# Where the node sums are zeroed, and a memset behind every second edge gather: a graph and expert kernel on one core

## The reference, cut to what matters

```
x = x + gnn(layernorm(x), z, src, dst, sh, ele)
    h   = linear(x_n) * z ;  s = linear_skip(x_n) * z
    w   = silu(ele @ fc_w0) @ fc_w1                # 50000 x 256, one row per edge
    mid = products of w, h[src] and sh             # 50000 x 512
    y   = segment_sum(mid, dst)                    # 3125 x 512
    out = c_s * s + c_x * linear2(y) * z
x = x + ffn(layernorm(x))
    shared expert (gelu) on all nodes + the two best of 8 experts, weighted
```

## Time and profile before

| | us |
|---|---|
| median of three runs | 1373.57 (1373.14 to 1381.37) |
| the profiled execution | 1377.12 |
| its span, first to last instruction | 1375.2 |
| first gather to last gather | 65.19 to 799.03 |
| mean granted TensorE clock | 0.895 of full |

### The profile page before, as it was taken

One profiled execution on the slowest core, in us unless ns is written; L12 is line 12 of the kernel. 1 busy time (PEld: TensorE's weight loads), 2 busy tenths in 40 slices (PEclk: granted clock), 3 DMA queues, 4 the chain that ended last, 5 costly groups with the idle time before them and its releaser, 6 DMA issues. The chain is left out here.

```text
span 1375.2 us, 31654 instructions
## 1 busy us (share of the span) xinstructions
PE 1175.3 (85%) x8904; PEld 1008.7 (73%) x8904; DVE 769.0 (56%) x1951; ACT 726.8 (53%) x2357; POOL 634.2 (46%) x695
## 2 busy tenths in 40 slices
PE   5667888788888888878878887999799999999993
PEld 4445666667766666656756677999799999999993
DVE  5634555555555545545555567644357666676652
ACT  4535766566756656655746666445344444444431
POOL 4565555545545545445444510355224444455443
PEclk9869888878979888878888898999899999999997
DMA  8652323323323333323333336223324344443222
GB/s 292 191 163 82 103 72 114 115 82 105 99 92 105 95 99 111 105 86 110 97 92 93 98 109 216 89 77 112 102 59 101 54 97 105 108 105 73 43 40 31
DMA packets 86943, 141.64 MB, mean 103 GB/s; under 512 B 14926, under 2 KB 65422, under 8 KB 86480
## 3 DMA queue, kind: packets, MB, share of 16 engines
q0 software_dynamic: 31840, 67.39, 20.1%
q1 hardware_dynamic: 51104, 69.90, 15.2%
q10 hardware_dynamic: 3920, 3.41, 0.8%
HBM read 99.48 MB, written 30.95 MB: 95 GB/s over the span
## 5 line engine op out<-in xcount | busy, mean ns | idle before, releaser
L748 POOL DMA_INDIRECT x_wlo<-h_tab,src_sb x392 | 376.5, 960 | 365.0 <-DVE hot L897 155.3
L779 ACT ACTIVATE hots<-hot,sh_all 128x64 f32<-128x64 f32 x1568 | 383.9, 336 | 0.0
L1103 PE MATMUL psY<-prod,hots 128*64 128x128 f32 x2352 | 345.9, 311 | 13.1 <-issue 12.4
L1103 PEld LDWEIGHTS psY<-prod,hots 128*64 128x64 f32 x2352 | 312.9, 160 | 28.0 <-issue 28.0
L1099 PE MATMUL psY<-prod,hots 128*64 128x256 f32 x784 | 273.4, 472 | 10.4 <-issue 10.1
L925 DVE SCALAR_TENSOR_TENSOR y_sb<-psY,mask,y_sb 128x256 f32 x196 | 85.7, 478 | 264.9 <-remote 235.0
L1864 ACT ACTIVATE q_hf<-q_psA,x_b 128x256 f32<-128x256 f32 x232 | 110.2, 475 | 186.7 <-PE q_psA L1380 166.5
L1087 PE MATMUL psW<-fc_w,hid 64*128 64x256 f32 x784 | 154.5, 447 | 63.6 <-issue 51.7
L769 ACT ACTIVATE hid<-psE 128x256 f32<-128x256 f32 x98 | 37.3, 380 | 279.3 <-remote 140.5
L1087 PEld LDWEIGHTS psW<-fc_w,hid 64*128 64x128 f32 x784 | 83.3, 204 | 121.4 <-issue 89.8
L1807 POOL DMA_INDIRECT out_rows<-q_ob,q_index x56 | 91.4, 1633 | 152.0 <-issue 98.0
(11 more groups left out here) (243 smaller groups left out, 2253.6 us busy)
## 6 DMA issues: line engine op xcount, KB each, us to landing
x_raw<-in_w SPq DMA_DIRECT2D x18, 1024.0 KB, 6.0
x_wlo<-h_tab,src_sb POOLq DMA_INDIRECT x392
u_y<-y_sb SPq DMA_DIRECT2D x11, 512.0 KB
y_sb<-y_sb SPq DMA_DIRECT2D x2, 2176.0 KB, 13.8
x_sb<-in_x SPq DMA_DIRECT2D x5, 640.0 KB, 6.0
h_tab<-x_raw ACTq DMA_DIRECT2D x5, 640.0 KB, 4.9
base_d<-s_sb SPq DMA_DIRECT2D x5, 640.0 KB, 3.7
cols_hi<-xT_d SPq DMA_DIRECT2D x5, 640.0 KB, 4.4
```

The lines of the kernel that those rows point to most:

```text
L748: pool.indirect_dma_start(out=rows[t % RING][:, c, :, :].rearrange("p a u -> p (a u)"), out_offset=None, in_=h_tab, in_offset=bass.Indirec ...
L779: ins = nc.scalar.activation(hots[p][:, c, n, :], hot[p][:, c, :], ACT.Copy, scale=sh_all[:, at(j), c, n:n + 1].rearrange("p o n -> p (o n)"))
L1103: ins = nc.tensor.matmul(side[:, k::3 - k, :][:, 0:2, :], hots[p][:, c, k + 1, :], prod[p][:, c, 4::k + 1, :][:, 0:2, :], start=(c == 0 an ...
```

## The change

1. The two transfers that zero 34 rows of `y_sb` leave SP's queue in the node block, with the wait on them at the block's end.
2. In the edge block POOL fills rows 18 to 34 with a memset before it waits for `h_tab`, and ACT writes rows 35 to 51 with one copy of rows 0 to 16, behind its table load and before its first silu. DVE waits for both before step 0.
3. Behind columns 1 and 3 of every step POOL fills `blank`, a tile of 128x256 that nothing reads before it is filled again at the end, waits until that memset is done, and goes on. That is 196 memsets and 196 waits.

```diff
@@ node_block, SP
-            sp.wait_ge(pool_step, 11)
-            for i in range(2):
-                first = BLOCKS + 2 - ZERO * (i + 1)
-                sp.dma_start(y_sb[:, first:first + ZERO, :], y_sb[:, 0:ZERO, :]).then_inc(y_zero, 16)
             sp.wait_ge(span_done, 1)
...
-            sp.wait_ge(y_zero, 32)
@@ edge_block, GpSimd
             link = chain_of(pool, pool_step)
+            pool.memset(y_sb[:, BLOCKS + 2 - 2 * ZERO:BLOCKS + 2 - ZERO, :], 0.0).then_inc(y_zero, 1)
             pool.wait_ge(h_out[0], 16 * (NG // 2 + 2))
...
                         ).then_inc(row_in[t % ITER], 16)
+                        if c % 2 == 1:
+                            pool.memset(blank[:], 0.0).then_inc(paused, 1)
+                            pool.wait_ge(paused, (r * T + t) * 2 + c // 2 + 1)
+                            pool.sem_inc(gather_turn, 1)
@@ edge_block, ScalarE
             nc.scalar.activation(warm[:], iota_row[:, 0:1], ACT.Silu)
+            nc.scalar.activation(y_sb[:, BLOCKS + 2 - ZERO:, :], y_sb[:, 0:ZERO, :], ACT.Copy).then_inc(y_zero, 1)
@@ edge_block, VectorE
                 one_hot(r, 0, 0)
+                dve.wait_ge(y_zero, 2)
                 for q in range(ITER):
```

More of the change, by code:

```diff
@@ L213, in node_block @@
         pool_step, dve_step = sem("pool_step"), sem("dve_step")
-        span_done, y_zero = sem("span_done"), sem("y_zero")
+        span_done = sem("span_done")
         passed = sem("passed")
@@ L525, in edge_block @@
     MOST = PAIR + 1
+    ZERO = (BLOCKS + 2) // 3
     assert T - ITERS * ITER == 2 and PAIR == 2 and CHUNK * 2 == ITER and NT == 2 * ITERS + 1
@@ L586, in edge_block @@
         hots_done, seg_done, y_done = sem("hots_done"), sem("seg_done"), sem("y_done")
-        gather_turn = sem("gather_turn")
+        gather_turn, paused = sem("gather_turn"), sem("paused")
         whi_part, wlo_part = sem("e_whi_part"), sem("e_wlo_part")
@@ L597, in edge_block @@
                                                                      "u_cols_free"))
-        u_go = sem("u_go")
+        u_go, y_zero = sem("u_go"), sem("y_zero")
         block = ctx.enter_context(nc.Block())
```

## The result

| us | before | changed |
|---|---|---|
| median of four runs | 1373.36 (1370.73 to 1381.37) | 1323.97 (1323.68 to 1328.81) |
| profiled execution, its span | 1377.12, 1375.2 | 1323.68, 1321.7 |
| mean granted TensorE clock | 0.895 | 0.916 |

The ratio is 0.9627 [0.9594, 0.966]: the changed kernel is 49.4 us faster on this chip, where 40 were forecast. The number of this chip is not on record. The experiments will show that the gain was seen only where the kernel before takes 1373 us.

The account below looks back on a forecast made before the run. PE was taken as the bound, slowed when gathers follow without a break. From the profiled 1377.1 us, -3.6 (node block), 0 (zeroing) and -37 (pauses) gave 1336.5; the median stands 3.55 lower, so 1333 us, range 1280 to 1395.

Parts of the forecast that it names:

- partial relief: Edge block: the forecast itself, 196 pauses end part of PE's stall and save 37 us; 1333 us, chance 0.43.
- full relief: Edge block rival: pauses break gather runs before the stall, POOL paces; saves 100 to 122 us, about 1263; chance 0.14.
- two signs of being wrong: Edge stage: first-to-last gather span not falling by 15 us or more, or DVE waiting for gathered rows mid-stage.
- Part 1: Node block: without the `y_sb` transfers DVE's second group starts earlier and ACT's wait goes; -3.6 us, between -3.6 and 0.
- Part 2: Start of edge block: zeroing by POOL's memset and ACT's copy is covered by waits; 0 us, from 0 to +7.7.
- Part 3, the pause's length: POOL, behind columns 1 and 3: each pause adds 0.38 to 0.68 us, taken as 0.5.
- The test written ahead: POOL's gather starts across a pause: nearer 2.0 than 1.76 us apart would mean the assumed pause is too short.
- Part 3, the worth of a pause: Edge block: PE makes m = 8 passes per us in a pause, break-even 5.8; 0.19 us saved each, 196 save 37.
- POOL's stop at 6.24 us a step: Edge block: POOL's own time a step with 0.5 us pauses, which caps the saving at 122 us.
- The pauses change nothing: Edge block rival: stall does not hang on gather spacing, only part 1 is left; about 1370 us, chance 0.23.
- The pauses stretch the stall: Edge block rival: pauses bring only PE's stalled rate, 57 us dearer, less 3.6; about 1427 us, chance 0.20.
- if that cover is gone, the whole 98 us is on the path: Edge block: without POOL's 3.72 us of idle behind each run of eight, all 196 pauses of 0.5 us cost time.

Follow-up runs that it names:

- e1: Changed kernel without the four lines of the pause, so only the zero fill is moved: 1124.79 us on chip 15, before beside it 1132.62.
- e8: Changed kernel with each memset waited for only before the next one, two gathers later: 1363.80 us on chip 3, before beside it 1372.32.
- e2: Kernel before with the 196 pauses and nothing else: 1331.24 us on chip 15, before beside it 1132.62, ratio 1.176.
- e3: Changed kernel with the pause's fill cut from 128x256 to 128x1, wait kept: 1283.79 us on chip 15, before beside it 1132.62.
- e4: Changed kernel with one pause a step, behind column 3 only: 1231.55 us on chip 15, before beside it 1132.62.
- e6: Changed kernel with one pause a step behind column 3 and its fill cut to 128x1: 1207.30 us on chip 2, before beside it 1131.53.
- e13: Kernel before with gathers fetching 64 floats for each edge instead of 256, sums not the reference's: 1136.00 us on chip 15, before beside it 1134.62.
- b2: Kernel before, unaltered, run again on chip 2 for its trace: 1130.29 us, ratio 0.9989.

## Why the prediction was right, and where it was not

**The time** (1323.97, forecast 1333, range 1280 to 1395) and the direction were right, for the chip of the first measurement. The mechanism was another than the forecast's: it took partial relief with PE still the bound, and what came was full relief with POOL the bound, at a price that made the two sums nearly equal. That they are so near is luck: 37 us were forecast for the pauses as a share of the stall, and what came was all of it less POOL's new floor. Of the two signs of being wrong that the prediction names, one did not come (the first-to-last gather span fell by 37.1 us, over its 15), and the other did: DVE waits 255.2 us for gathered rows in the middle of the stage, "which would mean that POOL's path has become the bound".

**Part 1** was mis-sized: -3.6 us forecast, -6.8 in the profile, -7.8 in e1. `span_d` is issued at 16.80 us directly behind the weights, DVE's second group starts at 17.45 instead of 19.37, so 1.9 us earlier and not 1.27, ACT's wait for `h_tab` is gone, and the slowest landing there took 6.0 us, not 10.3. Both terms were too small: the first store of `h_tab` starts at 23.44 instead of 26.87, so 3.4 us earlier where 1.27 were taken, and the third at 37.38 instead of 44.18, which is 3.4 more where the wait was priced at 2.3. (The two transfers hold 4.46 MB, not 4.35; nothing hangs on it.)

**Part 2** was right at 0. The fill took 3.73 us (3.7 taken) and ended at 57.24, 1.15 us before the first gather. It cost nothing: the first gather starts 8.17 us behind the start of the last store of `h_tab` before (57.02 to 65.19) and 8.16 after (50.22 to 58.38). ACT's copy took 3.81 us (4 taken), and DVE's first product still waited 2.77 us for rows.

**Part 3, the pause's length.** This step failed: "A pause therefore adds from 0.38 us to 0.68 ... I take 0.5." It adds 1.0. The working took the wait and the next gather's start as one more 0.30 us gap. The gap behind the memset is 0.97 us, and e8, with the same memset and no wait for its own end, has 0.16 there. So the wait for the memset just issued costs about 0.8 us. One reading is that POOL prepares the next gather only behind the wait; no row shows the preparing. The test written ahead ("if that is nearer 2.0 than 1.76 us, my pause is too short") came out at 2.26.

**Part 3, the worth of a pause.** "I take 9 early and 7 late, m = 8" rested on pauses of 0.5 us; with 1.0 us the stall does not begin. The longest chance pause held 18 passes, and one of 1.64 us held 15. Against the 5 of 1.26 us that row alone gives m = 10/0.38 = 26, so 15 was not the upper bound that the prediction calls it. The forecast put POOL's stop at 6.24 us a step (the first gather's 0.20 us come once in a run of two steps, so its own rows gave 6.14); with the true pause the same sum (4 x 1.26 + 2 x 1.0) gives 7.04, and (7.49 - 7.04) x 98 = 44 us. At the 7.11 measured, first to last gather gained 37.1; the edge stage as a whole gained 46.0.

**The rivals.** *Full relief*, at a chance of 0.14, had the mechanism right, and its 1263 us the same pause too short: with 7.04 us a step it comes to 1370 - 44 = 1326. *The pauses change nothing* is refuted on the first chip. Its ground is the rule of the Trainium skill (SBUF — State Buffer, the section "SBUF: two separate sides") that engine ports and DMA ports are disjoint and PE never waits. The traces where before takes 1131 to 1135 us agree: PE is busy 344 of 350 us with gathers back to back. The earlier trace rows and e8 do not, and there the measurement decides; that SBUF's ports are where PE is held up no run shows. *The pauses stretch the stall* fell for the chip it was written for: the edge stage became 46 us shorter, not longer. Yet the same change is 17% slower on chip 2, by no rival of mine, and five of the six chips of the runs have no stall: with none to relieve, 2.0 us of pauses a step are on POOL's path, and POOL was at its floor already. The prediction had said it in one clause, "if that cover is gone, the whole 98 us is on the path"; with 1.0 us a pause it is 196 us, and e2, the pauses alone, measured 199.

**What would have shown it** in the profile before: nothing. A trace from one chip can't tell that another has no stall.

**Still open.** What holds PE up on chips like chip 3 is not named by any row. It is not the clock alone: the stall of the earlier trace rows is at clock 1.00. One reading is that transfers as such crowd PE out. Against it, the same 104 GB/s stand in the earlier trace rows beside 8.5 passes per us and beside 2.4. And on a chip of the other kind, e1 from 78 to 80 us, the DMA engines are full at 412 GB/s and PE stays busy at full clock:

```profile
78.00:80.00 2.00, 2.00 (x14) 1.15 (x12) 1.50 (x4) 1.74 (x8) 1.60 (x2) 1.00 1.03 412
```

Whether e1, e3, e4 or e6 would beat the changed kernel where before stalls was not seen: none of them ran there. If it is the unbroken rest that counts, the shortest that frees PE lies between 0.50 us (e8) and 1.31 us behind a pair; if it is the rate, between one gather in 1.35 us and one in 1.76. Of the versions run, e1, the zero fill alone, is the best on the common kind of chip: 0.6% faster than before (0.994 [0.9917, 0.9963]).

## What to carry to other kernels

Price a pause by the distance from one start to the next with the wait on it, not by the filler's busy time: here 0.33 us of memset made 1.0 us, and times 196 that moved the bound to the engine that pauses. Compute that engine's new floor per step with the dear end of the pause, since that floor and not the relief is what the kernel will run at. And a change whose gain rests on a stall that no row explains is measured on several chips first: the part that needs no stall is kept (the zero fill: 7.8 us on the common kind in e1, and the first gather 6.8 us earlier on the stalling kind), the part that does was worth about -41 us, by difference, on one kind and +199 on the other.

## What was not expected of the hardware

- The same program takes 1372 us on one chip and 1131 to 1135 on five others. The difference is in the edge block: 7.49 against 5.09 us a step; PE makes 6.3 against 9.4 passes per us.
- The kernel with the pauses takes 1324 us on both kinds, 1323.97 where before took 1373 and 1324.69 on chip 2.
- A wait of POOL for the memset it has just issued costs 0.8 us: 0.97 us from the memset's end to the next gather with it, 0.16 without (e8). The fill's size adds only its own time (128x1: 0.11 us of fill, a pair 3.28 us; 128x256: 0.33 us, 3.52).
- An indirect gather of 128 rows takes POOL 0.97 us with rows of 256 bytes (e13) as with rows of 1 KB (b2).
- The granted clock is 0.89 in the changed kernel's edge stage, between its two levels of 1.2 and 2.4 GHz, and 1.00 in before's on chip 2. There PE is busy 344 of 350 us, here 405 of 500, with waits for products in between:

```profile
150.00:650.00 500.00, 404.92 (x3421) 325.63 (x3416) 286.62 (x595) 329.63 (x1278) 314.52 (x420) 0.89 0.36 106
```
